# A two-layer recurrent block on one core: keys turned on TensorE, SSD scores by 64 keys, TensorE's rounds in a loop, and another order in the last pair

## Chip, core and metric

The kernel runs on one core of a Trainium2 chip. The metric is device time in microseconds (us) of one execution; lower is better. Several executions are timed and their median is given. One more execution is run under the hardware profiler, and every row below is from that one.

## What is computed

The input is 2048 tokens of 256 channels in fp32 (two sequences of 1024). Two layers follow each other, each a sequence mixer gated by a feed-forward network:

```
xn = layernorm(x);  x = x + rwkv6(xn) * silu(ffn_2to4(xn))     # layer 0
xn = layernorm(x);  x = x + ssd(xn)   * silu(ffn(xn))          # layer 1
```

Layer 0's mixer is RWKV-6 with 4 heads of 64: per head `y_t = r_t (S + u k_t v_t^T)` and `S = d_t S + k_t v_t^T`, with a decay `d_t` for each token and channel. Its hidden layer keeps the 2 largest of each 4 units. Layer 1's mixer is SSD: each of 8 heads of 64 channels owns 512/8 = 64 of the rows of a sequence flattened over token and head, in chunks; inside a chunk `scores = (C B^T) * L`, where `L` is the exponential of differences of a cumulative sum and zero for a key behind its query. Everything is fp32.

## The kernel before

The tokens go through in 8 tiles of 256. A round works on a pair: tile `a` in layer 0 and tile `b` (the one before it) in layer 1. There are nine rounds: the first (tile 0 in layer 0 alone), pairs 1 to 7, and a final one (tile 7 in layer 1 alone). Each of the five engines has its own program, `one(a, b)`, written out by hand in the order in which that engine does its work; semaphores tie the engines together. PSUM has 8 banks of 512 columns; the table `FILLS` lists which product goes into which bank in which order, `open_bank` waits until the bank's previous content is freed, `wait_filled` and `wait_freed` are the readers' waits. The counts that they wait for are constants, or expressions of a loop register where the rounds are in a loop. `passed` is a semaphore that nobody waits for; incrementing it gives a wait an instruction to sit on.

On SyncE, GpSimd, ScalarE and VectorE pairs 1 to 6 are a hardware loop (`Fori`), and pair 7 and the final round are written out behind it. On TensorE all nine rounds are written out (`for n in range(1, NT)`).

In a pair TensorE does, among much else and in this order: the feed-forward products of pair unit 2 (`project_p(a, 2, ...)`), `high_levels` (the intra-chunk products of layer 0 at distances 32 and 64; L1651 and L1707), `scores(0)` and `scores(1)` (L1763), `project_p(a, 3, ...)`, `states` (L2002), `within` (L1778), `chunk_states` (L1933, keys times values of layer 0 for the state), `across` (L1789), `outputs` (L1724 to L1735), and then the large feed-forward products of `b`. An fp32 product is two MATMUL records in the trace, a transpose one.

Layer 0's keys are kept by channel (`kT`); `chunk_states` needs them by token (`k0n`, which is the buffer `mixed_w`). In a pair this goes through VectorE and DRAM: `keys_to_end` (L1120 to L1123) writes the keys times their decay, transposes them by 32x32 blocks and SyncE's `key_rows` (L397, L400) stores them with 8 DMAs and loads them with one. In the first round TensorE transposes them instead (`keys_turned`, L1915).

`ssd_scores` multiplies, for each chunk of 128 rows and each sequence half `s`, all 128 keys with all 128 queries. The two halves `s` take different rows of the array (0 to 63 and 64 to 127). VectorE multiplies the result with `L` (`decayed_scores`, L1343) and frees the bank. The keys' side of a chunk is loaded from DRAM as rows: `cs_pos`, `Xrow` and `Brow` (the last two inside the buffer `hidB`), one DMA each.

In the first round TensorE runs `kept_busy` (L1967), 39 small products that nobody reads, ahead of `rank_mix` (L1816), which waits for VectorE's `rank_inputs` (L1174).

Of the kernel before, what the change touches and what calls it, by code (L numbers as in the profile page):

```python
# [17 lines left out]
F32 = mybir.dt.float32  # L18
# [6 lines left out]
P = 128  # L25
TOKENS, BATCH, C = 2048, 2, 256
T = 256
# [26 lines left out]
FILLS = [["mix_w", "dw", "w0", "mix_g0", "L0", "M0", "p3g", "kv", "F0"],  # L54
         ["p0g", "mix_k", "w1", "mix_g1", "L1", "M1", "p3u", "yT"],
# [5 lines left out]
         ["X1", "C0", "sc2", "ys0", "n1g", "n3g", "p1g"]]  # L61
BANKS = len(FILLS)
# [53 lines left out]
def build_block(nc, A):  # L116
    with ExitStack() as ctx:
# [3 lines left out]
        def sem(name):  # L121
# [4 lines left out]
             if n not in ("x", "out", "x_turned", "n_dram", "row_dram", "cs_dram", "b_dram", "x_dram", "k_dram", "w_mix2b", "w_dec2")}  # L126
# [64 lines left out]

        k0_turned = mixed["k"][:, :, :].rearrange("p a b -> p (a b)")
# [78 lines left out]
        k_blocks = sem("k_blocks")  # L271
        k_stored = sem("k_stored")
        k_rows = sem("k_rows")
# [99 lines left out]
        def _(sp_):  # L373
# [17 lines left out]
            def key_rows(a):  # L391
                wait(k_rows, a.count(16, 0))
                wait(k_blocks, a.count(1, 0))
                to = A["k_dram"].rearrange("(j a h i b) -> i h a j b", a=32, h=CH, i=4, b=32)
                for i in range(4):
                    for h in range(CH):
                        sp_.dma_start(to[i, h], k0_turned[32 * i:32 * i + 32, h * T:(h + 1) * T].rearrange(  # L397
                            "p (j b) -> p j b", b=32)).then_inc(k_stored, 16)
                wait(k_stored, a.count(128, 0))
                sp_.dma_start(k0n[:, :, :].rearrange("p a b -> p (a b)").rearrange("p (q c) -> p q c", q=NQ),  # L400
                              A["k_dram"].rearrange("(q p c) -> p q c", p=P, c=C)).then_inc(k_rows, 16)

# [29 lines left out]
            def one(a, b, last=False):  # L432
# [11 lines left out]
                if b:  # L444
# [3 lines left out]
                    wait(X_rows, b.count(16, 16))  # L448
# [4 lines left out]
                    wait(cs_loaded, b.count(48, 16))  # L453
# [4 lines left out]
                    sp_.dma_start(cs_pos[:, :], cs_dram.rearrange("(c p) -> p c", p=P),  # L458
                                  allow_slow_non_contiguous=True).then_inc(cs_loaded, 16)
# [5 lines left out]
                    sp_.dma_start(Xrow.rearrange("p q c d -> p (q c) d"),  # L465
# [1793 lines left out]
```

## Time and profile before

| | before |
|---|---|
| median of 3 runs | 716.09 us (715.89 to 716.32) |
| the profiled execution | 717.52 us |
| its span, first to last instruction | 715.7 us |
| TensorE (PE) busy | 702.5 us, 98% |
| TensorE weight loads (PEld) | 597.9 us, 84% |
| VectorE (DVE) busy | 496.1 us, 69% |
| ScalarE (ACT) busy | 338.1 us, 47% |
| GpSimd (POOL) busy | 76.7 us, 11% |
| granted TensorE clock | 1.000 of full speed |
| share of PE in the chain that ended last | 87% |

The profiled execution lies 1.4 us over the median and 1.8 us over its own span. Names of a row: line of the kernel, engine, operation, output<-inputs, shape, count. A start time is in us from the start of the span; the second number is the time from the group's first start to its last end. Ends of matmuls are modelled and overlap with the next, so the length of a piece of TensorE's work is read as the difference of two starts.

### The profile page before, as it was taken

What the parts mean: (1) busy time and instruction counts of PE and PEld (TensorE: products, weight loads), DVE (VectorE), ACT (ScalarE), POOL (GpSimd) and SP (SyncE); (2) the same over time, 40 slices, a digit from 0 to 9 for tenths busy, and PEclk for the clock granted to TensorE, in tenths of its full rate; (3) what the DMA queues carried; (4) which work ended last, traced back from release to release, by engine and by line L of the source; (5) the groups of instructions that cost most, each with busy time, mean ns of one, the idle gap of its engine ahead of it and who ended that gap; (6) DMA issues with size and microseconds to landing.
All of it is one profiled execution on the core that took longest, in us unless ns stands there. A gap on an engine that the chain in (4) does not pass through costs nothing.

```text
span 715.7 us, 18156 instructions
## 1 busy us (share of the span) xinstructions
PE 702.5 (98%) x7010; PEld 597.9 (84%) x7010; DVE 496.1 (69%) x1214; ACT 338.1 (47%) x671; POOL 76.7 (11%) x85
## 2 busy tenths in 40 slices
PE   7999999999999999999999999999999999999998
PEld 5777788888888788887888878888788888888887
DVE  5995988528884488755896568954789529895133
ACT  1423782147711586206852068421783237821790
POOL 6301011101110011100111001110011100110020
PEclk9999999999999999999999999999999999999999
DMA  7911460125501364012720236202370025601370
GB/s 231 408 44 30 136 103 18 22 82 143 96 2 30 102 128 83 16 30 89 149 61 16 52 120 110 47 15 74 104 128 23 16 77 136 105 12 25 122 120 16
DMA packets 139572, 59.46 MB, mean 83 GB/s; under 512 B 119728, under 2 KB 131312, under 8 KB 137968
## 3 DMA queue, kind: packets, MB, share of 16 engines
q1 hardware_dynamic: 139504, 58.44, 33.9%
q8 instruction: 57, 0.93, 0.6%
q14 instruction: 11, 0.09, 0.0%
HBM read 44.18 MB, written 14.24 MB: 82 GB/s over the span
## 4 chain that ended last, share of the span: by engine, by line
PE 87%; DVE 5%; issue 3%; DMA 2%; ACT 2%; SPq 1%; POOL 0%; DVEq 0%; POOLq 0%; ACTq 0%
PE psum L1542 68%; PE psum L1651 2%; PE psum L1763 2%; PE psum L1778 2%; ACT BC L626 1%; PE psum L1596 1%; PE psum L1621 1%; PE psum L1816 1%; PE psum L2002 1%; PE psum L1684 1%; PE psum L1863 1%; PE psum L1633 1%; PE psum L1789 1%; PE psum L1735 1%; PE psum L1724 1%
## 5 line engine op out<-in xcount | busy, mean ns | idle before, releaser
L626 ACT ACTIVATE BC<-psum 64x256 f32<-64x256 f32 x128 | 81.6, 637 | 1.9 <-PE psum L1542 0.2
L1542 PE MATMUL psum<-xn1T,sb_n_gate 128*128 128x256 f32 x256 | 61.3, 382 | 0.0
L1542 PE MATMUL psum<-xn1T,sb_n_up 128*128 128x256 f32 x256 | 60.5, 379 | 0.0
L1542 PE MATMUL psum<-xnT,sb_f_gate 128*128 128x256 f32 x240 | 57.8, 383 | 0.0
L1542 PE MATMUL psum<-xnT,sb_f_up 128*128 128x256 f32 x240 | 57.0, 379 | 0.0
L1542 PEld LDWEIGHTS psum<-xn1T,sb_n_gate 128*128 128x128 f32 x256 | 48.0, 190 | 6.8
L1542 PEld LDWEIGHTS psum<-xn1T,sb_n_up 128*128 128x128 f32 x256 | 48.2, 190 | 6.3
L757 ACT ACTIVATE thFB<-psum 128x512 f32<-128x512 f32 x8 | 4.8, 597 | 102.1 <-PE psum L1542 102.1
L1542 PEld LDWEIGHTS psum<-xnT,sb_f_up 128*128 128x128 f32 x240 | 45.2, 189 | 6.8 <-issue 0.3
L1542 PEld LDWEIGHTS psum<-xnT,sb_f_gate 128*128 128x128 f32 x240 | 44.7, 189 | 7.2 <-DVE xnT L1205 0.2
L1542 PE MATMUL psum<-sb_n_down,hidB 128*128 128x256 f32 x224 | 49.5, 379 | 0.0
L1542 PEld LDWEIGHTS psum<-sb_n_down,hidB 128*128 128x128 f32 x224 | 42.6, 190 | 5.8
L577 POOL TENSOR_SCALAR_AFFINE_SELECT cs_row<-cs_row 128x2048 f32<-128x2048 f32 x8 | 16.1, 2006 | 277.1 <-DVE xn_turned L1012 251.9
L1542 PE MATMUL psum<-sb_f_down,hid 128*128 128x256 f32 x192 | 42.4, 379 | 0.0
L1542 PEld LDWEIGHTS psum<-sb_f_down,hid 128*128 128x128 f32 x192 | 36.5, 190 | 5.0
L652 ACT ACTIVATE cs_row<-cs_row,cs_col 128x128 f32<-128x128 f32 x128 | 38.9, 392 | 0.0
L924 DVE SCALAR_TENSOR_TENSOR hid<-th,psum 128x512 f32<-128x512 f32 x23 | 15.7, 685 | 24.0 <-PE psum L1542 24.0
L1542 PE MATMUL psum<-sb_w_X,xn1T 128*128 128x256 f32 x128 | 31.9, 392 | 0.0
L583 POOL TENSOR_TENSOR cs_half<-cs_half,BC 128x1024 f32<-128x1024 f32 x8 | 19.1, 2383 | 115.4 <-ACT cs_half L721 115.4
L1542 PE MATMUL psum<-xn1T,sb_w_B 128*128 128x256 f32 x128 | 31.0, 385 | 0.2
L1542 PE MATMUL psum<-xn1T,sb_w_res 128*128 128x256 f32 x128 | 30.8, 385 | 0.0
L740 ACT ACTIVATE mixed_v<-mixed_k 128x512 f32<-128x512 f32 x8 | 5.0, 630 | 54.4 <-DVE mixed_k L1248 54.4
(265 smaller groups left out, 1494.4 us busy)
## 6 DMA issues: line engine op xcount, KB each, us to landing
cs_row<-cs_dram SPq DMA_DIRECT2D x8, 1024.0 KB, 5.0
x_dram<-gate SPq DMA_DIRECT2D x8, 512.0 KB, 2.8
cs_half<-cs_dram SPq DMA_DIRECT2D x16, 256.0 KB, 5.8
hidB<-x_dram SPq DMA_DIRECT2D x8, 512.0 KB, 5.7
b_dram<-B_turned SPq DMA_DIRECT2D x32, 128.0 KB, 3.5
hidB<-b_dram SPq DMA_DIRECT2D x8, 512.0 KB, 4.2
X<-in_x SPq DMA_DIRECT2D x9, 256.0 KB, 2.9
XT<-in_x_turned SPq DMA_DIRECT2D x8, 256.0 KB, 2.9
```

The costliest lines, as they stand in the source:

```text
L577: g.affine_select(out=cs_row[:, :, :], in_=cs_row[:, :, :], compare_op=ALU.is_ge, fill=NEG, base=0, pattern=[[0, NQ * SCH], [1, P]], chann ...
L583: g.tensor_tensor(cs_half[:, :], cs_half[:, :], BC[:, 1, :, :].rearrange("p t h -> p (t h)"), ALU.mult).then_inc(Cdec_ready, 1)
L626: ins = a_.activation(cols[:, par, 2 * pair:2 * pair + 2, :], src[64 * par:64 * par + 64, :, s, :], ACT.Identity)
L652: ins = a_.activation(cs_row[:, n, :], cs_row[:, n, :], ACT.Exp, bias=cs_col[:, n:n + 1])
L924: free(d.scalar_tensor_tensor(out=to, in0=buf[:, :], scalar=2.0, in1=ps(t, name + "u")[:, :], op0=ALU.mult, op1=ALU.mult), t, name + "u")
L1542: ins = t_.matmul(ps(t, name)[first_row:first_row + rows, col:col + n], w, x, start=(k == 0), stop=(k == len(ws) - 1))
L1596: ins = t_.matmul(ps(t, "F0")[:, q * C:(q + 1) * C], hid[:, m, q * P:(q + 1) * P], W["f_down"][:, m * C:(m + 1) * C], start=(m == 0 and q ...
L1621: ins = t_.matmul(ps(t, "mix_" + f)[:, h * T:(h + 1) * T], W["w_mix2a"][r, h * P:(h + 1) * P], aT[r, :], start=True, stop=True)
L1633: ins = t_.matmul(ps(t, f"mix_g{q}")[:, h * P:(h + 1) * P], W["w_mix2b"][r, h * P:(h + 1) * P], aT4[r, :], start=True, stop=True)
L1651: ins[e] = t_.matmul(lev_pair[64 * hf:64 * hf + 64, e, first + g * 32:first + (g + 1) * 32], keys[r, c:c + 64], q, start=True, stop=True)
L1763: ins[s] = t_.matmul(ps(t, names[s])[:, i * P:(i + 1) * P], Bf[r, c * P:(c + 1) * P], Cf[r, c * P:(c + 1) * P], start=True, stop=True)
L1778: t_.matmul(y_out(t, s, c, par), Xrow[:, s, c, :], m[:, par, :], start=(c == 0), stop=(c == 0), skip_group_check=True)
```

## The change

1. **Keys.** `keys_to_end`, `key_rows` and the buffer in DRAM go. In each pair TensorE transposes the keys (`keys_turned`) once VectorE has multiplied them with their decay (`last_update`), and ScalarE copies them from PSUM (`copy(a, k0n, "k0T", NQ)`).
2. **Scores.** Each chunk is done by 64 keys: the first 64 keys with all 128 queries, the last 64 with the 64 queries behind them. The output rows of odd chunks are exchanged, so the first half of one chunk and the second half of the next lie in the same rows of PSUM. Keys therefore stand in another order in odd chunks: `cs_pos`, `Xrow` and `Brow` are each loaded by three DMAs (`KEY_ROWS`) in place of one, and GpSimd masks `cs_row` with three operations in place of one.
3. **Order in a pair.** `high_levels` goes ahead of `project_p(a, 2, "g")`, `chunk_states` right behind the scores, `outputs` ahead of `across`. VectorE's order follows.
4. **Loop.** TensorE's pairs 1 to 6 are a hardware loop (`rounds(pe, one)`); 23 increments of `passed` ahead of `out_1` go.
5. **Pair 7.** `out_0` stands right behind `down_part(a, 1, 4, 8)`; ScalarE does `out_scaled` ahead of the sigmoid of the down product, VectorE `residual_0` ahead of `hidden_n(b, 2)`.
6. **First round.** `kept_busy` has 19 products in place of 39.

```diff
+KEY_ROWS = [(slice(0, P), 0, slice(0, P)), (slice(0, 64), 1, slice(64, P)), (slice(64, P), 1, slice(0, 64))]
...
@@ sync
-            def key_rows(a):
...
-                        sp_.dma_start(to[i, h], k0_turned[32 * i:32 * i + 32, h * T:(h + 1) * T].rearrange(
-                            "p (j b) -> p j b", b=32)).then_inc(k_stored, 16)
...
-                    sp_.dma_start(Brow.rearrange("p q c d -> p (q c) d"),
-                                  b_dram.rearrange("(c p d) -> p c d", p=P, d=SD)).then_inc(B_rows, 16)
+                    keys = b_dram.rearrange("(c two p d) -> p c two d", two=2, p=P, d=SD)
+                    for to, r, from_ in KEY_ROWS:
+                        sp_.dma_start(Brow.rearrange("p q (c two) d -> p (q c) two d", two=2)[to, :, r, :],
+                                      keys[from_, :, r, :]).then_inc(B_rows, 16)
                     if a:
-                        key_rows(a)
                         token_rows(a)
@@ gpsimd
-                    g.affine_select(out=cs_row[:, :, :], in_=cs_row[:, :, :], compare_op=ALU.is_ge, fill=NEG, base=0,
-                                    pattern=[[0, NQ * SCH], [1, P]], channel_multiplier=-1).then_inc(cs_masked, 1)
+                    for last, r, two, base in ((P, slice(0, P), 0, 0), (P, slice(0, P), 1, 64), (64, slice(0, 64), 1, -64)):
+                        m = by_two[r, :, two, :]
+                        ins = g.affine_select(out=m, in_=m, compare_op=ALU.is_ge, fill=NEG, base=base,
+                                              pattern=[[0, NQ * SCH // 2], [1, P]], channel_multiplier=-1)
...
@@ scalar
                     ffn_tanh(a, "p2", th[0], th_ready, "p0")
+                    copy(a, k0n[:, :, :], "k0T", NQ)
                     L_exps(1)
@@ vector
                     B_by_block(1)
-                    end_args()
+                    dve.wait_ge(out_stored, b.count(16, 16))
...
                     level_next(a, 5)
+                    end_args()
+                    low_taken(a)
                     gate_0()
-                    low_taken(a)
-                    keys_to_end(a)
+                    high_taken(a)
+                    last_update(a)
                     res_gate(0)
                     res_gate(1)
-                    high_taken(a)
-                    last_update(a)
                     decayed_scores(0)
-                    decayed_scores(1)
+                    states_0()
+                    B_decayed()
+                    for n in (2, 1, 3):
+                        decayed_scores(n)
                     hidden_p(a, 2)
-                    B_decayed()
...
                     states_1()
-                    states_0()
                     hidden_p(a, 3)
@@ tensor, ssd_scores
-                        ins[s] = t_.matmul(ps(t, names[s])[:, i * P:(i + 1) * P], Bf[r, c * P:(c + 1) * P],
-                                           Cf[r, c * P:(c + 1) * P], start=True, stop=True)
+                    for first in range(2):
+                        k, at = slice(c * P + 64 * first, c * P + 64 * first + 64), 64 * (first ^ (c % 2))
+                        for s in range(NQ):
+                            r = half_rows(s)
+                            ins[s] = t_.matmul(ps(t, names[s])[at:at + 64, i * P + 64 * first:(i + 1) * P], Bf[r, k],
+                                               Cf[r, c * P + 64 * first:(c + 1) * P], start=True, stop=True)
@@ tensor, one, last pair
                         close_bank(down_part(a, 1, 4, 8), a, "F0")
+                        out_0()
                         up_n(b, 2)
-                        out_0()
                         gate_n(b, 3)
                     up_n(b, 3)
-                    for _ in range(23):
-                        pe.sem_inc(passed, 1)
                     out_1()
...
-                    kept_busy(["mix_w", "mix_k"], 39)
+                    kept_busy(["mix_w", "mix_k"], 19)
...
-            one(Tile(None, 0, first=True), None)
-            for n in range(1, NT):
-                one(Tile(None, n), Tile(None, n - 1))
-            one(None, Tile(None, NT - 1, last=True))
+            rounds(pe, one)
```

TensorE's program in a pair, before, from `project_p(a, 2, "u")` to the start of `outputs` (counts are products; `thFB,xn` and `rT,kT` are `high_levels`, `BC` the scores, `hidB` the states):

```order
L1542 MATMUL psum<-xnT,sb_f_up 128x256 x4
L1542 MATMUL psum<-xnT,sb_f_gate 128x256 x4
L1651 MATMUL psum<-thFB,xn 64x32 x16
L1707 MATMUL psum<-rT,kT 64x64 x8
L1763 MATMUL psum<-BC 128x128 x16
L1542 MATMUL psum<-xnT,sb_f_gate 128x256 x4
L1542 MATMUL psum<-xnT,sb_f_up 128x256 x4
L2002 MATMUL psum<-hidB 64x64 x14
L1778 MATMUL psum<-cs_row,hidB 64x64 x32
L1933 MATMUL psum<-v,mixed_w 64x64 x8
L1789 MATMUL psum<-cs_half,S 64x64 x28
L1724 MATMUL psum<-S,rT 64x64 x16
```

The same place in the changed program, inside the loop, up to the first chunk of the scores:

```order
L1535 MATMUL psum<-xnT,sb_f_up 128x256 x4
L1524 REGISTER_ALU
L1663 REGISTER_ALU
L1644 MATMUL psum<-thFB,xn 64x32 x16
L1694 REGISTER_ALU
L1700 MATMUL psum<-rT,kT 64x64 x8
L1535 MATMUL psum<-xnT,sb_f_gate 128x256 x4
L1912 MATMUL psum<-ident,kT 128x128 x4
L1760 MATMUL psum<-BC 64x128 x2
L1760 MATMUL psum<-BC 64x64 x2
```

`high_levels` now has a dense product on either side, four transposes are new, and a chunk's 2 products of 128 keys are 4 of 64 keys, 2 of them with 64 queries. Instructions on registers are new: there are 37 of them and 7 waits written as ISA instructions in a round.

VectorE's program at the same place, before (L1010 and L1012 make level 5, L1033 and L1027 are `low_taken`, L1120 to L1123 `keys_to_end`, L1311 `res_gate`):

```order
L1210 SCALAR_TENSOR_TENSOR gT<-gT,psum 128x512
L1033 COPY_PREDICATED own<-masks,psum 128x128x2
L1033 COPY_PREDICATED own<-masks,psum 128x64x4
L1033 COPY_PREDICATED own<-masks,psum 128x32x8
L1027 COPY_PREDICATED own<-masks,psum 128x8x16 x2
L1116 REGISTER_ALU
L1120 TENSOR_TENSOR mixed_w<-kT,dec 128x4x64
L1121 COPY mixed_w<-kT 128x4x64
L1123 STREAM_TRANSPOSE mixed_k<-mixed_w 128x512
L1309 ISA
L1311 SCALAR_TENSOR_TENSOR gate<-gate,psum 128x512 x2
```

And in the changed program, from `low_taken` on:

```order
L1030 COPY_PREDICATED own<-masks,psum 128x8x16 x2
L1196 SCALAR_TENSOR_TENSOR gT<-gT,psum 128x512
L339 REGISTER_ALU
L1036 COPY_PREDICATED own<-masks,psum 128x8x32
L999 TENSOR_TENSOR kT<-kT,dec 128x4x64
L1000 TENSOR_TENSOR rT<-rT,dec 128x4x64
L1295 ISA
L1297 SCALAR_TENSOR_TENSOR gate<-gate,psum 128x512 x2
L334 REGISTER_ALU
L1329 TENSOR_TENSOR cs_row<-cs_row,psum 128x512
L1207 SCALAR_TENSOR_TENSOR S<-S,dec,psum 128x64 x4
```

The transpose and one copy are gone, the gate stands behind `low_taken`, and the states of layer 0 (L1207, before L1221) come right behind the first `decayed_scores`.

## Rows read from the trace of the kernel before

**Rows 1.** The page's first part: busy us (share of span) xinstructions

```profile
PE 702.5 (98%) x7010; PEld 597.9 (84%) x7010; DVE 496.1 (69%) x1214; ACT 338.1 (47%) x671; POOL 76.7 (11%) x85
```

**Rows 2.** Timeline of PE, pair 4: start us, us, what, [idle before <-releaser]

```profile
359.86 0.67 PE L1651 MATMUL psum<-thFB,xn 64*64 64x32 f32 x32
360.95 2.06 PE L1763 MATMUL psum<-BC 64*128 64x128 f32 x32
362.93 2.00 PE L1542 MATMUL psum<-xnT,sb_f_gate 128*128 128x256 f32 x8
...
366.59 1.03 PE L2002 MATMUL psum<-hidB 128*64 128x64 f32 x28
...
369.35 0.65 PE L1933 MATMUL psum<-v,mixed_w 128*64 128x64 f32 x16
369.92 1.05 PE L1789 MATMUL psum<-cs_half,S 64*64 64x64 f32 x56
371.16 0.69 PE L1724 MATMUL psum<-S,rT 64*64 64x64 f32 x32 [0.18 <-DVE S L1221]
```

**Rows 3.** Timeline of PE, pair 4: four transposes between dense products

```profile
388.36 0.60 PE L1610 MATMUL psum<-ident,mixed_k 128*128 128x128 f32 x4
388.80 1.89 PE L1542 MATMUL psum<-xn1T,sb_n_up 128*128 128x256 f32 x8
```

**Rows 4.** Timeline of PE, pair 4: products of 64 rows by 64 columns with 96 columns

```profile
348.36 0.89 PE L1684 MATMUL psum<-rU,kT 64*64 64x96 f32 x32
349.07 0.62 PE L1651 MATMUL psum<-mixed_r,mixed_w 64*64 64x32 f32 x32
```

**Rows 5.** Timeline of PE, pair 1: the wait for the turned keys

```profile
107.86 2.07 PE L1778 MATMUL psum<-cs_row,hidB 128*64 128x64 f32 x64
110.67 0.69 PE L1933 MATMUL psum<-v,mixed_w 128*64 128x64 f32 x16 [0.75 <-DMA mixed_w<-k_dram]
```

**Rows 6.** Timeline of DVE, pair 4: the gate and the end of `low_taken`

```profile
355.80 0.69 DVE L1210 SCALAR_TENSOR_TENSOR gT<-gT,psum 128x512 f32<-128x512 f32 x1 [0.38 <-ACT gT L714]
...
358.10 0.50 DVE L1027 COPY_PREDICATED own<-masks,psum 128x128 f32<-128x128 int8 x2
```

**Rows 7.** Timeline of ACT, pair 4: `L_exps(1)`

```profile
363.00 2.44 ACT L652 ACTIVATE cs_row<-cs_row,cs_col 128x128 f32<-128x128 f32 x8
```

**Rows 8.** Timelines at the end of pair 4: PE around the 23 increments and at the round's end, then ACT

```profile
393.98 1.89 PE L1542 MATMUL psum<-xn1T,sb_n_up 128*128 128x256 f32 x8
395.71 3.62 PE L1542 MATMUL psum<-sb_w_sout,gate 128*128 128x256 f32 x16
...
412.99 1.02 PE L1816 MATMUL psum<-mixed_w,sb_w_mix 128*128 128x256 f32 x4
...
406.27 0.60 ACT L757 ACTIVATE thFB<-psum 128x512 f32<-128x512 f32 x1 [13.14 <-PE psum L1542]
```

**Rows 9.** Timelines of PE and of DVE, first round

```profile
10.41 1.36 PE L1967 MATMUL psum<-ident 64*64 64x32 f32 x78
11.71 1.13 PE L1816 MATMUL psum<-mixed_w,sb_w_mix 128*128 128x256 f32 x4
...
10.06 1.04 DVE L1174 SCALAR_TENSOR_TENSOR mixed_w<-dxT,sb_vecs,xnT 128x256 f32<-128x256 f32 x2
```

**Rows 10.** Timelines of PE in pair 7 and the final round, and of DVE in the final round

```profile
650.35 1.99 PE L1542 MATMUL psum<-sb_w_rkvgo,mixed_w 128*128 128x256 f32 x8 [0.60 <-DVE mixed_w L1268]
...
666.47 0.63 PE L1805 MATMUL psum<-xn1T,sb_w_dt 128*32 128x128 f32 x8 [0.32 <-DMA xn1T<-n_dram]
...
697.67 1.03 PE L2002 MATMUL psum<-hidB 128*64 128x64 f32 x28
...
700.97 1.05 PE L1789 MATMUL psum<-cs_half,S 64*64 64x64 f32 x56 [0.37 <-issue]
...
695.33 1.16 DVE L1333 TENSOR_TENSOR hidB<-hidB,to_end 128x448 f32<-128x448 f32 x2 [1.20 <-DMA hidB<-b_dram]
```

**Rows 11.** DMA issues: out<-in, count, KB each, median us from issue to landing

```profile
n_dram<-xn_turned SPq DMA_DIRECT2D x56, 32.0 KB, 1.7
```

More of the change, by code:

```diff
@@ L125, in build_block @@
         W = {n: sb("sb_" + n, list(A[n].shape)) for n in A
-             if n not in ("x", "out", "x_turned", "n_dram", "row_dram", "cs_dram", "b_dram", "x_dram", "k_dram", "w_mix2b", "w_dec2")}
+             if n not in ("x", "out", "x_turned", "n_dram", "row_dram", "cs_dram", "b_dram", "x_dram", "w_mix2b", "w_dec2")}
         W["w_mix2b"], W["w_dec2"] = sb("sb_mix2b", [NQ * DMIX, C]), sb("sb_dec2", [NQ * DDEC, C])
@@ L447, in one @@
                     sp_.sem_inc(passed, 1)
-                    wait(X_rows, b.count(16, 16))
+                    wait(X_rows, b.count(48, 16))
                     sp_.dma_start(x_dram.rearrange("(q p n) -> p q n", q=NQ, p=P), Xnat).then_inc(X_stored, 16)
@@ L452, in one @@
                     sp_.sem_inc(passed, 1)
-                    wait(cs_loaded, b.count(48, 16))
+                    wait(cs_loaded, b.count(80, 16))
                     wait(cs_rows_loaded, b.count(16, 16))
@@ L464, in one @@
                     wait(X_stored, b.count(16, 32))
-                    sp_.dma_start(Xrow.rearrange("p q c d -> p (q c) d"),
-                                  x_dram.rearrange("(c p d) -> p c d", p=P, d=SD)).then_inc(X_rows, 16)
-                    wait(B_rows, b.count(16, 16))
+                    keys = x_dram.rearrange("(c two p d) -> p c two d", two=2, p=P, d=SD)
+                    for to, r, from_ in KEY_ROWS:
+                        sp_.dma_start(Xrow.rearrange("p q (c two) d -> p (q c) two d", two=2)[to, :, r, :],
+                                      keys[from_, :, r, :]).then_inc(X_rows, 16)
+                    wait(B_rows, b.count(48, 16))
                     wait(B_blocks, b.count(2, 2))
@@ L802, in one @@
                     ffn_tanh(b, "n1", thB[1], None)
-                    ffn_tanh_0()
-                    out_scaled()
-                    ffn_tanh(b, "n2", thB[0], None, "n0")
+                    if a.reg is not None:
+                        ffn_tanh_0()
+                        out_scaled()
+                        ffn_tanh(b, "n2", thB[0], None, "n0")
+                    else:
+                        ffn_tanh(b, "n2", thB[0], None, "n0")
+                        out_scaled()
+                        ffn_tanh_0()
                     ffn_tanh(b, "n3", thB[1], None, "n1")
@@ L1757, in ssd_scores @@
                     open_bank(t, name)
+                    pe.sem_inc(passed, 1)
                 ins = [None] * NQ
@@ L1799, in one @@
             def one(a, b):
-                first_a, first_b = not b, a and b and b.off == 0
+                first_a, first_b = not b, a and b and (a.reg is not None)
                 def steps_product(bank, h):
@@ L1938, in outputs @@
                     wait_freed(pe, a, "kv")
-                    if a.first:
-                        wait_freed(pe, a, "L0")
-                    wait_freed(pe, a, "L1" if a.first else "M1")
+                    for e in range(2):
+                        wait_freed(pe, a, f"{'L' if a.first else 'M'}{e}")
                     pe.wait_ge(q0_ready, a.count(1, 1))
@@ L2048, in one @@
                     project_p(a, 2, "u")
+                    high_levels(a)
                     project_p(a, 2, "g")
-                    high_levels(a)
+                    keys_turned()
                     scores(0)
                     scores(1)
+                    chunk_states()
                     project_p(a, 3, "g")
@@ L2056, in one @@
                     within()
-                    chunk_states()
+                    outputs()
                     across()
-                    outputs()
                     ffn_n(b, 0)
```

87 lines of the change are left out of this document (32 added, 55 removed).

## The prediction

> **What bounds the kernel now.** I read the page's first part first: TensorE (PE) is busy 98% of the span and no other engine over 69% [rows 1]. So the question is what TensorE's own program costs, and where it waits. Next comes TensorE's timeline of one pair in the middle, where the reader is to see that each group starts as the one before it lets go: two dense groups lie 1.73 us apart [rows 8], and the only idle time in the part that the change rewrites is 0.18 us ahead of `outputs` [rows 2]. [...] Then come the waits that occur once: 0.75 us in pair 1 [rows 5], 0.60 us in pair 7 and 0.32 us and 0.37 us in the final round [rows 10], and the products of the first round that only keep the engine busy [rows 9]. All that the other engines do is hidden, as long as it isn't late.
>
> **The change in a pair, part by part.**
>
> *Scores.* The 32 records take 360.95 to 362.93, 1.98 us [rows 2]. The new ones are 64 records of 64 rows by 64 columns, half with 128 queries and half with 64, 96 in the mean. The nearest row has just that shape and 96 columns: 32 records in 0.71 us, 22 ns each [rows 4]. 64 of them give 1.42 us, which is the lower bound. The upper bound is that a 64-query product doesn't run beside the 128-query products of its neighbour chunk; then a chunk takes what its 128-query products take, as now, 1.98 us. The rows of odd chunks are exchanged, so each quarter of the array gets 128 and 64 queries in turn, and I take the lower bound plus 0.1 for entering from a dense product: 1.5 us, that is -0.5.
>
> *Transposes.* Four transposes between dense products cost 388.80 - 388.36 = 0.44 us [rows 3]: +0.44. They stand on the path, since all of TensorE's program does.
>
> *Order.* `high_levels` now has dense products on both sides. What entering and leaving costs is read from the two dense groups between scores and states: 366.59 - 362.93 = 3.66 us where twice 1.73 is 3.46: +0.20. It could be nothing, if the scores behind the transposes start as quickly as they now do behind `high_levels`, or 0.3. `chunk_states` costs 369.92 - 369.35 = 0.57 us [rows 2] wherever it is, and I take it as moved for nothing. `outputs` no longer follows `chunk_states` through VectorE's update of the state, so its 0.18 us of waiting and what goes with it end: -0.2.
>
> Sum of a pair: -0.5 + 0.44 + 0.20 - 0.2 = -0.06 us; for seven pairs -0.4. Bounds of a pair: -0.35 to +0.55.
>
> *What hides the rest.* Each new wait has to be met in time. (1) `high_levels` wants its banks 1.73 us earlier, at about 358.1. VectorE's `low_taken` ends at 358.10 + 0.50 = 358.60, but the gate (0.69 us, 0.38 us idle ahead of it) goes behind it [rows 6], so it ends near 357.6: met with some 0.4 us to spare. (2) The transposes want the keys at about 361. `high_levels` ends near 359.2 (it lasts 1.09 us [rows 2]), and VectorE needs two operations of some 0.4 us behind it; met by a dense group. (3) `chunk_states` wants ScalarE's copy at about 363. The copy goes ahead of `L_exps(1)`, which starts at 363.00 now [rows 7] and could start two microseconds earlier, since `high_levels` ends that much earlier; the scores (1.5 us) cover the copy's 0.6. If that cover were gone, 0.6 us a pair would show. (4) The 9 DMAs of the keys leave SyncE's queue; in their place 2 each are added for `cs_pos`, `Xrow` and `Brow`. In a pair these land behind work of several microseconds. GpSimd's mask, three operations in place of one, ends ahead of `end_args`, which now stands behind level 5. All at nothing. (5) VectorE loses a transpose and a copy (1.0 us), so nothing behind it gets later.
>
> *Pair 1.* There `chunk_states` waits 0.75 us for the keys from DRAM, and starts 2.81 us behind `within` [rows 5]; the DMA goes: -0.8.
>
> *The loop.* I cost it at nothing. TensorE's instructions are issued ahead of the engine: the 23 semaphore increments between 393.98 and 395.71 leave no gap, the distance is the 1.73 us of a dense group [rows 8]. The same hides the 44 register instructions and ISA waits of a round, and means that taking the 23 away gains nothing. The last wait ahead of the branch back is for the bank that ScalarE's L757 frees at 406.27 + 0.60 = 406.87; the engine is busy with what was issued until 412.99 [rows 8]. So a stall of the branch stays hidden up to 6.1 us.
>
> [...]
>
> *First round.* 78 records of `kept_busy` run from 10.41, and `rank_mix` starts at 11.71; VectorE has its input ready at 10.06 + 1.04 = 11.10 [rows 9]. With half of the products `rank_mix` can start 0.1 to 0.2 us behind 11.10: -0.4. At worst nothing is left of it (a later wait for VectorE in that round), at best 0.6.
>
> *Pair 7.* `out_0` waits 0.60 us for the gated output now [rows 10], and `out_scaled` stands behind the sigmoid (0.6 us) on ScalarE. Ahead of it the input is ready that much earlier, but `out_0` is wanted 1.73 us earlier too, so part of the wait stays: -0.3. The whole chain behind it (residual, norm, turn, DRAM) starts some 2 us earlier, and so the final round's first wait, 0.32 us for `xn1T` [rows 10], ends: -0.3.
>
> *Final round.* The scores are 0.5 us shorter here too, but this round is fed by DMA: VectorE idles 1.20 us for `Brow`, has it decayed at 695.33 + 1.16 = 696.49, and TensorE starts the states at 697.67 [rows 10]. Three DMAs in place of one for `Brow` (and for two loads ahead of it in the same queue) may land 0 to 1.5 us later. And `across` waits 0.37 us for VectorE's chain of states already. I take -0.1, between -0.5 and +1.0.
>
> **Sum.** -0.4 (seven pairs) - 0.8 - 0.4 - 0.6 - 0.1 = -2.3 us. The profiled execution took 717.52 us, so 715.2 in its place; it lies 1.4 us over the median, and the median of the changed kernel should be 716.09 - 2.3 = 713.8 us.
>
> **The rivals.** What can be told from no change here is 0.2%, 1.4 us: faster is below 714.7, slower above 717.5.
>
> *The forecast's mechanism, with more gain.* The pairs come out 0.3 us shorter each (scores at 1.42 us, no cost of entering and leaving): -2.1 more, 711.7 us. For it: TensorE is the bound, and what it saves counts in full. Against it: the transposes are paid in each pair. Chance 0.14.
>
> *The same.* The pair costs 0.2 us more than I have it (a wait for ScalarE's copy or more time at each change of shape), seven times +1.4 us: 715.2 us; or the final round loses 1.0 to `Brow` and the first round gives nothing: the same place. Chance 0.24.
>
> *Slower: the small products of a chunk don't run beside the large ones.* Place: `ssd_scores`. Twice as many products, a chunk takes what its 128-query products take, 1.98 us, and the transposes come on top. +0.48 us in eight rounds, +3.8: 717.6 us. It decides from about 0.46 us a round on. For it: one product follows the other in program order, and unequal neighbours occur in no row. Against it: products on different quarters overlap fully when they are equal (22 ns a record [rows 4]). Chance 0.12.
>
> *Slower: the branch back isn't hidden.* Place: TensorE between `project_p` of the next tile and `rank_mix`. [...] It decides once 0.8 us shows at each branch. [...] Against it: 6.1 us of cover. Chance 0.10.
>
> *The forecast.* 713.8 us, by itself 712.7 to 714.6. Chance 0.40.
>
> **How the numbers follow.** Faster: 0.40 + 0.14 = 0.54. Within 0.2%: 0.24. Slower: 0.12 + 0.10 = 0.22. The range leaves out the unhidden branch above and the far end of the largest gain below: 711.3 to 717.8 us.
>
> **What the changed profile would show.** The scores' group starts and the next group starts 1.5 us later (right) or 2.0 us later (the third rival). Four transposes of `kT` in a pair with 0.44 us to the next start and no idle time ahead of them, nor ahead of `chunk_states`. The distance from `project_p(a, 2, "u")` to the first dense product behind `across` within 0.3 us of today's. No idle time at the loop's branch: `rank_mix` 1.73 us behind the last dense group's start. No wait for a DMA in pair 1. `rank_mix` of the first round near 11.3. In the final round the states right behind the dense group, or idle with `hidB<-b_dram` as the releaser. The prediction is wrong if idle time shows in each pair, since everything there counts seven times.

## The result, and the profile after

The changed kernel takes **718.85 us**, the median of 5 executions (718.06 to 720.36), beside 716.32 us for the kernel before, timed again next to it in 5 executions (715.89 to 717.66): ratio **1.0033, 95% interval 1.0019 to 1.0047**. It is slower, where I forecast faster. The profiled execution took 718.1 us (span 716.4) beside 717.52 (span 715.7), so of the 2.5 us between the medians the two spans show 0.7.

The page's first part, of the kernel after:

```profile
PE 703.2 (98%) x7254; PEld 596.2 (83%) x7254; DVE 491.9 (69%) x1200; ACT 343.2 (48%) x678; POOL 85.9 (12%) x101
```

This answers to [rows 1]: TensorE is the bound as before, at 98%. GpSimd has more to do. Next, TensorE's timeline of the kernel after: a branch back, pair 4, and pair 7 (start, duration, line, shapes, and in brackets idle time with what ended it).

```profile
149.23 1.71 PEld L1535 LDWEIGHTS psum<-xnT,sb_f_gate 128*128 128x128 f32 x8
149.44 1.90 PE L1535 MATMUL psum<-xnT,sb_f_gate 128*128 128x256 f32 x8
...
150.96 1.70 PEld L1535 LDWEIGHTS psum<-xnT,sb_f_up 128*128 128x128 f32 x8
151.17 1.89 PE L1535 MATMUL psum<-xnT,sb_f_up 128*128 128x256 f32 x8
...
153.16 0.51 PEld L1813 LDWEIGHTS psum<-mixed_w,sb_w_mix 128*128 128x128 f32 x3 [0.50 <-issue]
153.17 0.69 PE L1813 MATMUL psum<-mixed_w,sb_w_mix 128*128 128x256 f32 x2
...
356.33 1.90 PE L1535 MATMUL psum<-xnT,sb_f_up 128*128 128x256 f32 x8
358.34 0.67 PE L1644 MATMUL psum<-thFB,xn 64*64 64x32 f32 x32
358.82 0.68 PE L1700 MATMUL psum<-rT,kT 64*64 64x64 f32 x16
359.44 2.00 PE L1535 MATMUL psum<-xnT,sb_f_gate 128*128 128x256 f32 x8
361.27 0.60 PE L1912 MATMUL psum<-ident,kT 128*128 128x128 f32 x4
361.80 1.57 PE L1760 MATMUL psum<-BC 64*64 64x128 f32 x64
363.30 0.69 PE L1926 MATMUL psum<-v,mixed_w 128*64 128x64 f32 x16
363.92 2.00 PE L1535 MATMUL psum<-xnT,sb_f_gate 128*128 128x256 f32 x8
...
615.58 1.89 PE L1535 MATMUL psum<-xnT,sb_f_up 128*128 128x256 f32 x8
617.99 0.67 PE L1644 MATMUL psum<-thFB,xn 64*64 64x32 f32 x32 [0.52 <-DVE own L1030]
```

Two lines of the kernel before belong beside them, the dense groups ahead of `high_levels` and ahead of `rank_mix` in pair 4; the next groups start at 359.86 [rows 2] and at 412.99 [rows 8]:

```profile
358.03 1.89 PE L1542 MATMUL psum<-xnT,sb_f_gate 128*128 128x256 f32 x8
...
411.26 1.89 PE L1542 MATMUL psum<-xnT,sb_f_up 128*128 128x256 f32 x8
```

Three things are to be seen. (a) `rank_mix` (L1813) stands 153.17 - 151.17 = 2.00 us behind the last dense group's start, where the kernel before has 412.99 - 411.26 = 1.73. At the five branches back the distance is 2.00, 2.19, 1.94, 1.78 and 1.84 us, and the four first products behind each take 0.10 us longer; at the sixth, which isn't taken, it is 1.73. Together 1.09 + 0.50 = 1.6 us. (b) `high_levels` (L1644) starts 2.01 us behind the start of a dense group that lets go after 1.82 (so it was in all seven pairs of the kernel before, 359.86 - 358.03 above); over the seven pairs it is 2.27, 2.02, 2.00, 2.01, 2.00, 1.99 and 2.41, 2.0 us in all. (c) The rest of pair 4 is what I forecast: scores 1.50 us, transposes 0.53.

```profile
L364 ACTq COMPARE_BRANCH  x6: 40/45/53, 151.5 to 584.7; - x6
L364 PEldq COMPARE_BRANCH  x6: 83/3682/3983, 149.1 to 582.3; - x6
```

And the register instruction ahead of TensorE's last dense group before the first branch, the only one of line L1524 from 146 to 150 us:

```profile
L1524 PEldq ALU_OP  x1: 32/32/32, 147.3 to 147.3; - x1
```

TensorE's branch back takes 3.6 to 4.0 us when it is taken, and 0.08 the sixth time. ScalarE's, with a shorter body, takes 0.05.

And where (b) comes from, VectorE and GpSimd in the timeline of the kernel after, in pair 4 and then pair 7:

```profile
351.38 1.31 DVE L1312 STREAM_TRANSPOSE B_turned<-BC 128x512 f32<-128x512 f32 x2 [0.33 <-DVE own L1099]
352.61 0.72 DVE L1013 TENSOR_TENSOR xn<-thB,dec 128x256 f32<-128x256 f32 x1
...
353.45 0.41 DVE L1013 TENSOR_TENSOR thFB<-xn_turned,dec 128x256 f32<-128x256 f32 x1
...
357.46 0.50 DVE L1030 COPY_PREDICATED own<-masks,psum 128x128 f32<-128x128 int8 x2
...
611.96 1.12 DVE L1013 TENSOR_TENSOR xn<-thB,dec 128x256 f32<-128x256 f32 x1
```

```profile
349.40 1.09 POOL L571 TENSOR_SCALAR_AFFINE_SELECT cs_row<-cs_row 128x1024 f32<-128x1024 f32 x1 [38.10 <-DVE xn_turned L1015]
350.72 2.33 POOL L571 TENSOR_SCALAR_AFFINE_SELECT cs_row<-cs_row 128x1024 f32<-128x1024 f32 x2 [0.23 <-POOL cs_row L571]
...
609.24 3.56 POOL L571 TENSOR_SCALAR_AFFINE_SELECT cs_row<-cs_row 128x1024 f32<-128x1024 f32 x3 [38.32 <-DVE xn_turned L1015]
```

The same place in the kernel before, GpSimd in pair 4:

```profile
349.45 2.01 POOL L577 TENSOR_SCALAR_AFFINE_SELECT cs_row<-cs_row 128x2048 f32<-128x2048 f32 x1 [37.88 <-DVE xn_turned L1012]
```

The mask lasted until 351.46; in three operations it lasts until 353.05 in pair 4 and 612.80 in pair 7. VectorE's first product of level 4, 0.42 us by itself, starts ahead of that end, and each time ends 0.28 us behind it: 353.33 and 613.08. (0.28 is less than 0.42: either a part of it was done beside the mask, or GpSimd's ends are recorded late; no run tells which.) What is late there is late in `low_taken` too, which ends at 357.46 + 0.50 = 357.96; `high_levels` starts 0.38 us behind that.

### The profile page after: what moved, and what is told of

The parts are those of the page before. It is cut to its first block, busy times and chain, and to the rows that moved or that the text cites. A ratio compares the mean times of both kernels' runs of the same rounds, so it can differ in the third digit from the quotient of the medians.

```text
span 716.4 us, 18704 instructions
## 1 busy us (share of the span) xinstructions
PE 703.2 (98%) x7254; PEld 596.2 (83%) x7254; DVE 491.9 (69%) x1200; ACT 343.2 (48%) x678; POOL 85.9 (12%) x101
## 4 chain that ended last, share of the span: by engine, by line
PE 91%; DVE 5%; issue 2%; ACT 1%; POOL 0%; DVEq 0%; POOLq 0%; ACTq 0%
PE psum L1535 71%; PE psum L1644 2%; PE psum L1775 2%; PE psum L1760 2%; PE psum L1614 1%; PE psum L1813 1%; PE psum L1994 1%; PE psum L1786 1%; PE psum L1589 1%; PE psum L1677 1%; PE psum L1860 1%; PE psum L1626 1%; PE psum L1926 1%; PE psum L2173 1%; PE psum L1717 1%
## 5 line engine op out<-in xcount | busy, mean ns | idle before, releaser
L571 POOL TENSOR_SCALAR_AFFINE_SELECT cs_row<-cs_row 128x1024 f32<-128x1024 f32 (+1 forms) x24 | 26.2, 1092 | 283.2 <-DVE xn_turned L1015 253.3
```

Of the source, the lines that this page charges most:

```text
L571: ins = g.affine_select(out=m, in_=m, compare_op=ALU.is_ge, fill=NEG, base=base, pattern=[[0, NQ * SCH // 2], [1, P]], channel_multiplier=-1)
```

## The experiments

Theory: two things that I had put at nothing cost the time, the branch back on TensorE and the longer mask on GpSimd. Rivals: the body of a pair or the final round lost it, or the branch only shows in a profile. The runs were made in three batches, each beside the kernel before: 716.51 us in the first (part 1), 716.69 in the second (e4, e5, e7, e2h) and 716.47 in the third (e8 to e11). A difference of 0.2 us between runs of two batches says nothing.

**1. The loop.** The changed kernel again, written out, and hinted; and the loop alone in the kernel before.

> The changed kernel once more, beside the others on their chip: 718.9 us if the five timed executions were typical. In its first profile the five distances from the last dense group to rank_mix behind a branch back were 2.00, 2.19, 1.94, 1.78 and 1.84 us where 1.73 is the bare distance. If the stall is a fetch whose length varies, the new profile has other values at the same five places and all other distances unchanged to 0.05 us; if the loss lies in the body (the new wait ahead of high_levels, the final round), it repeats where it was.

> The changed kernel with TensorE's rounds written out again (nothing else undone). Theory (the branch back shows): the five places lose their excess, 1.09 us of distance and 5 x 0.10 us of slower first products in the profiled execution, up to 3.4 us if the timed executions stalled longer than the profiled one: 715.5 to 717.2 us, and executions as close together as those of the kernel before. Rival (the body of the pair and the final round cost it): no change, 718.5 to 719.0 us.

```diff
-            rounds(pe, one)
+            one(Tile(None, 0, first=True), None)
+            for n in range(1, NT):
+                one(Tile(None, n), Tile(None, n - 1))
+            one(None, Tile(None, NT - 1, last=True))
```

(three conditions that tell the first and the last pair by the loop's register go back to the tile's number with it)

> The kernel before with TensorE's rounds in a loop and nothing else (the 23 increments stay). Theory: the branches cost here what they cost in the changed kernel, 1.6 to 3.4 us: 717.9 to 719.7 us, spread over more than 1 us. Rival (body): 716.3 us. My prediction, loop at nothing: 716.3 us too.

```diff
-            one(Tile(None, 0, first=True), None)
-            for n in range(1, NT):
-                one(Tile(None, n), Tile(None, n - 1))
-            one(None, Tile(None, NT - 1, last=True))
+            rounds(pe, one)
```

(with the same three conditions by the register)

```diff
-        def rounds(eng, one):
+        def rounds(eng, one, **loop):
...
-            with eng.Fori(1, NT - 1) as it:
+            with eng.bass.Fori(1, NT - 1, engines=[eng.engine], **loop) as it:
...
-            rounds(pe, one)
+            rounds(pe, one, hint_back_edge=True)
```

Only TensorE's loop gets the hint.

| run | median us (executions) | ratio to before | interval |
|---|---|---|---|
| after_again | 718.35 (12) | 1.0024 | 1.0014 to 1.0035 |
| e1_unrolled | 721.99 (6) | 1.0063 | 1.0042 to 1.0084 |
| e2_loop_alone | 720.98 (6) | 1.0061 | 1.0041 to 1.0080 |
| e3_hint | 716.34 (12) | 1.0000 | 0.9990 to 1.0011 |

The hint gives back 2.0 us, as expected, and the loop alone makes the kernel before slower, by 4.5 us, which is more than I expected (717.9 to 719.7): the branch costs time. In after_again the five distances are 1.82, 2.25, 2.06, 2.11 and 1.91 us: the same places, other values, 1.5 us over the bare distance and 0.5 for the slower first products, 2.0 in all. The source line of the loop in e3_hint:

```profile
L364 PEldq BRANCH_PREFETCH_HINT  x6: 31/31/50, 65.2 to 494.4; - x6
L364 PEldq COMPARE_BRANCH  x6: 80/220/260, 148.9 to 580.4; - x6
```

The branch takes 0.22 us, `rank_mix` is 1.73 us behind the dense group at all five places, and the excess is gone. So the stall was the wait for the target's instructions, not the branch or its registers. The part of the page on DMA queues, first of the kernel after, then of e3_hint, says the same:

```profile
q8 instruction: 67, 1.10, 0.7%
```

```profile
q8 instruction: 22, 0.36, 0.2%
```

Without the hint a fetch starts 1.3 us behind each taken branch (150.38 us, branch at 149.12; it lands at 151.47, and the branch is over at 152.92, 1.45 us later), and blocks are fetched all through the loop; with it no instruction DMA of TensorE appears between 116.45 and 582.08 us.

But e1_unrolled missed my expectation: written out, the changed kernel is the slowest of all. Its timeline and its windows in pair 4 (windows: busy time and count of each engine, granted clock, DMA share):

```profile
350.12 0.52 PE L1644 MATMUL psum<-xn_turned,thB 64*64 64x32 f32 x22
352.37 0.41 PE L1644 MATMUL psum<-xn_turned,thB 64*64 64x32 f32 x10 [1.73 <-issue]
352.72 2.69 PE L1535 MATMUL psum<-xn1T,sb_w_res 128*128 128x256 f32 x8
```

```profile
350.00:352.00 2.00, 0.64 (x44) 0.53 (x36) 1.67 (x4) 1.97 (x4) 1.62 (x3) 1.00 0.06 8
352.00:354.00 2.00, 1.63 (x16) 1.44 (x17) 1.85 (x6) 1.95 (x4) 0.78 (x1) 0.97 0.31 49
354.00:356.00 2.00, 2.00 (x6) 1.61 (x5) 1.90 (x7) 0.83 (x2) 0.00 (x0) 0.50 0.68 98
```

In the middle of a level TensorE waits 1.73 us for nothing but its own instructions, up to 352.37; an instruction DMA was on its way from 349.62 to 350.99, so the work goes on 1.38 us behind its landing, much as at the branch (1.45). Behind that idle time the granted clock is 0.50 in 354 to 356 us, and the dense groups are 2.49 and 2.76 us apart where they are 1.83 and 1.73 at 1.00: another 1.7 us. An idle time of 1.21 us at 636 us in the same profile left it at 1.00.

Why there? The kernel before has 57 instruction DMAs of 16 KB for 14543 instructions on TensorE's queues, e1_unrolled 58 for 14894. That is 255 and 257 each; I take it as 256 (an estimate from these counts). A written-out round of the kernel before has 1792 instructions, 7 x 256, and its seventh fetch starts 72.0 to 72.8 us behind `rank_mix` in each of pairs 1 to 7: each round meets its fetches at about the same places. One of e1_unrolled has 1844, and the places walk by 52 a round (the seventh fetch at 74.5, 70.5 and 66.5 us in pairs 1 to 3), now and then into a stretch of small products.

**2. The mask, and its order on VectorE**, all on the hinted version (716.34 us).

> The hinted version of the changed kernel, with end_args moved from ahead of low_taken to behind it on VectorE (0.45 us of VectorE's time: 353.87 to 354.32 in the hinted profile). Theory (VectorE is late with low_taken, TensorE waits ahead of high_levels): the distance from project_p(a, 2, u) to the first product of high_levels falls from 1.99 to 1.82 us in six pairs, and in pair 7 from 2.41 to about 1.96: -1.4 us against the hinted version's 716.3, so 714.9 us. Rival (the wait moves to the next thing that VectorE owes, the gate or the update of level 6): 716.0 to 716.4 us.

```diff
-                    end_args()
                     low_taken(a)
+                    end_args()
                     gate_0()
```

> The hinted version with GpSimd's mask in one operation as before; the rows of odd chunks are then masked at the wrong places, so the output differs. Theory (GpSimd's three operations last 3.65 us instead of 2.01, reach into VectorE's first tensor_tensor of level 4, and hold it: 0.72 us in a middle pair and 1.11 in pair 7 where 0.42 is its time): that operation is 0.42 us again, VectorE is 0.3 us earlier in a pair and 0.7 in pair 7, and the wait ahead of high_levels goes: 714.6 to 715.0 us. Rival (the longer operation has another cause, such as its own operands): still 0.72 us, 716.3 us.

```diff
-                    for last, r, two, base in ((P, slice(0, P), 0, 0), (P, slice(0, P), 1, 64), (64, slice(0, 64), 1, -64)):
...
+                    g.affine_select(out=cs_row[:, :, :], in_=cs_row[:, :, :], compare_op=ALU.is_ge, fill=NEG, base=0,
+                                    pattern=[[0, NQ * SCH], [1, P]], channel_multiplier=-1).then_inc(cs_masked, 1)
```

> The hinted version, with GpSimd's second mask operation over queries 0 to 63 only (there is nothing to mask behind them for those keys): 512 columns in place of 1024 in that operation, the output as in the reference. Theory (the mask's third operation reaches into VectorE's first tensor_tensor of level 4 and makes low_taken late): the three end 0.5 us sooner, at about VectorE's start in a middle pair and 0.15 us into it in pair 7, so the operation takes 0.42 us again, the distance from project_p(a, 2, u) to high_levels is 1.82, and the time is that of the run with one mask, 714.7 us. Rival (something else in that run, such as its exp of other values, made it quick): 716.3 us.

```diff
-                        m = by_two[r, :, two, :]
+                        n = 64 if base == 64 else P
+                        m = by_two[r, :, two, 0:n]
...
-                                              pattern=[[0, NQ * SCH // 2], [1, P]], channel_multiplier=-1)
+                                              pattern=[[0, NQ * SCH // 2], [1, n]], channel_multiplier=-1)
```

e4_end_args: 720.16 us (6 executions; ratio 1.0045, 1.0032 to 1.0058), 3.8 us slower than e3_hint. Both expectations missed the time; the rival had it right that the wait moves, but it moves to what ScalarE owes, and grows. Its chain of waits, the first row, and a row of ScalarE's timeline:

```profile
PE psum L1912 <- ACT other L728: 3.4, 7, 0.9
```

```profile
358.05 0.21 ACT L733 ACTIVATE to_end<-to_end 128x16 f32<-128x16 f32 x1 [2.05 <-DVE to_end L1305]
```

`high_levels` no longer waits, but ScalarE stands 2.05 us idle for `end_args`, its exps and `other` copy come later, and the transposes wait for those. Both users of this stretch of VectorE are near their limit.

e5_one_mask: 714.65 us (9 executions; ratio 0.9972, 0.9962 to 0.9982), as expected; by itself it leaves open that other values made it quick, which the next run rules out. e8_hint_narrow_mask: **714.82 us** (713.96 to 715.59, 9 executions; ratio to the kernel before **0.9972, 0.9959 to 0.9984**), as expected too. GpSimd, VectorE and TensorE in the timeline of e8_hint_narrow_mask, pair 4:

```profile
349.19 1.89 POOL L572 TENSOR_SCALAR_AFFINE_SELECT cs_row<-cs_row 128x512 f32<-128x512 f32 x2 [0.23 <-POOL cs_row L572]
...
351.08 0.38 DVE L1014 TENSOR_TENSOR xn<-thB,dec 128x256 f32<-128x256 f32 x1
...
355.58 0.49 DVE L1031 COPY_PREDICATED own<-masks,psum 128x128 f32<-128x128 int8 x2
...
354.80 1.89 PE L1536 MATMUL psum<-xnT,sb_f_up 128*128 128x256 f32 x8
356.63 0.67 PE L1645 MATMUL psum<-thFB,xn 64*64 64x32 f32 x32
```

The mask ends at 351.08, VectorE's operation starts then and takes 0.38, and `high_levels` follows after 1.83 us; so it is in six pairs. In pair 7 the mask (606.80 to 609.92) still reaches into that operation, which takes 0.68 us, and the distance is 1.97 where I expected 1.82. Only half of one operation's columns was taken away; that it gives 1.5 us shows the collision, not GpSimd's work, to be the cost. This version beats both kernels.

**3. The terms that I had counted.**

> The hinted version with the scores by 128 keys, and with them the single DMAs and the single mask: the rest of the change alone. Theory (the scores give 0.48 us in each of eight rounds, 3.9 us, and their mask takes 1.5 us back through VectorE): 716.3 + 3.9 - 1.5 = 718.7 us, with no wait ahead of high_levels. Rival (what the scores give is lost behind them, in states, within or the final round): 716.5 to 717.2 us.

```diff
-                    for first in range(2):
...
-                            ins[s] = t_.matmul(ps(t, names[s])[at:at + 64, i * P + 64 * first:(i + 1) * P], Bf[r, k],
-                                               Cf[r, c * P + 64 * first:(c + 1) * P], start=True, stop=True)
+                    for s in range(NQ):
+                        r = half_rows(s)
+                        ins[s] = t_.matmul(ps(t, names[s])[:, i * P:(i + 1) * P], Bf[r, c * P:(c + 1) * P],
+                                           Cf[r, c * P:(c + 1) * P], start=True, stop=True)
```

(with one DMA each for `cs_pos`, `Xrow` and `Brow`, and the single mask, as in the kernel before)

> The kernel before with TensorE's loop and the hint, nothing else. Theory (the loop costs only the branch, and with the hint that takes 0.2 us and is hidden): 716.3 us, 715.8 if the instruction fetches that the hinted loop no longer shows had cost something. Rival (the register instructions of the loop cost too): 716.8 to 717.5 us. With e7 it gives the keys' part: e7 minus this is what transposes, order and pair 7 are worth; by my terms (+0.44 + 0.2 - 0.2 in a pair, -0.8, -0.4, -0.6) this is +1.3 us.

Its edit is that of e2_loop_alone and that of e3_hint together.

> The kernel before without its 23 semaphore increments, its only edit; rounds stay written out. My prediction (they are hidden, taking them away gains or costs nothing): 716.5 us. Rival: with them a written-out round is 1792 instructions, 7 x 256, and each instruction DMA brings 16 KB, 256 instructions, so each round meets its fetches at the same places; without them they drift by 23 instructions a round and fall, as in the run with the changed kernel written out (1844 a round), into stretches of small products: 717.5 to 719.5 us with idle time put down to issue.

```diff
-                    for _ in range(23):
-                        pe.sem_inc(passed, 1)
```

> e8_hint_narrow_mask with pair 7's order as before on TensorE, ScalarE and VectorE. By my term (0.3 for out_0 and 0.3 for xn1T) it is 0.6 us slower than that one: 715.3 us. By the profiles so far the new order is worth 0.1 to 0.3 us only, since out_0 still waits and the final round waits for the next thing: 714.9 us.

TensorE's part of its edit; ScalarE and VectorE go back in the same way:

```diff
-                        out_0()
                         up_n(b, 2)
+                        out_0()
                         gate_n(b, 3)
```

> e8_hint_narrow_mask with 39 rounds of kept_busy in the first round instead of 19. By my term it is 0.4 us slower: 715.1 us. Rival (rank_mix starts when its input is ready, whatever stands ahead of it): 714.7 us; rank_mix then starts as late with 19 as with 39, counted from the start of kept_busy.

```diff
-                    kept_busy(["mix_w", "mix_k"], 19)
+                    kept_busy(["mix_w", "mix_k"], 39)
```

| run | median us (executions) | ratio to before | interval |
|---|---|---|---|
| e7_old_scores | 718.23 (11) | 1.0020 | 1.0011 to 1.0029 |
| e2h_loop_hint_alone | 717.14 (12) | 1.0006 | 0.9997 to 1.0014 |
| e9_before_no_incs | 717.16 (12) | 1.0005 | 0.9995 to 1.0016 |
| e10_old_pair7 | 715.52 (12) | 0.9984 | 0.9974 to 0.9994 |
| e11_kept_busy_39 | 716.32 (12) | 0.9995 | 0.9985 to 1.0006 |

- *Scores.* e7_old_scores and e5_one_mask differ in the scores and their loads and share the single mask: 718.23 - 714.65 = 3.6 us, 0.45 a round. In its timeline the old form takes 363.40 - 361.42 = 1.98 us again, against 1.50.
- *Keys, order, first round, pair 7.* e7_old_scores minus e2h_loop_hint_alone is +1.1 us; my terms gave +1.3.
- *The loop with the hint.* e2h_loop_hint_alone came out at 717.14 us, in the range of its rival (register instructions cost), not at 716.3. But beside the 716.69 of its batch that is +0.45 with an interval from -0.2 to +1.0, and its profile (716.85 us) isn't longer than that of the kernel before: whether the registers cost anything is not shown.
- *The 23 increments.* By the time, taking them away makes no difference that can be told. The profile of e9_before_no_incs has more idle time put down to issue than the kernel before (1.8 us in five waits against 1.0 in four), so both expectations are in part right: the fetches do walk (the seventh of a round starts 73.9 us behind `rank_mix` in pair 1, then 77.0, 78.4, 80.7, 83.8 and 85.7 us), and mostly miss the small products here.
- *Pair 7's order.* +0.7 us without it, by the medians (0.6 by the profiles). With the old order `out_0` waits 0.60 us again; with the new one it still waits, 646.37 - 644.37 = 2.00 us against 1.73. That is worth 0.5 us where I had 0.3. The wait for `xn1T` shows in neither run, so its 0.3 us isn't in this difference. Another 0.25 us stands at pair 7's scores (1.79 us in e10_old_pair7 for 1.50), which the edit doesn't touch.
- *kept_busy.* e11_kept_busy_39 is 1.5 us slower, not 0.4. From the first of these products to `rank_mix` it is 1.29 us with 39 rounds and 0.73 with 19, and of these 0.56 us 0.10 are lost again to a later wait: 0.46. There is a second place, in pair 7, behind the loop, where all code has moved by 20 products and their loads. The fetch there ran from 605.97 to 607.07:

```profile
607.39 0.41 PE L1645 MATMUL psum<-xn_turned,thB 64*64 64x32 f32 x15
608.38 0.47 PE L1645 MATMUL psum<-xn_turned,thB 64*64 64x32 f32 x17 [0.58 <-issue]
```

The two profiles differ by 0.7 us in all (715.31 and 714.61), so of the 1.5 us between the medians 0.8 stand in no trace.

## Why the prediction was wrong, step by step

**Failed: "I cost it at nothing ... a stall of the branch stays hidden up to 6.1 us" (the loop).** The cover was mis-sized. I counted from the last wait ahead of the branch to the end of the engine's work, as if the sequencer were at the branch as soon as that wait ends. It comes there at 149.12, when 16 weight loads and 17 matmul records are still to start, some two dense groups, which end at 151.17 + 1.89 = 153.06: 3.9 us of cover. The branch takes 3.6 to 4.0 us (3682 ns in the middle), so it is nearly hidden and shows by 0.05 to 0.52 us. My rival of the branch that isn't hidden had the place, but needed 0.8 us at each branch to decide; shown are 0.3 to 0.4 in the mean in the two profiles, and 2.0 us in all by the medians (718.35 to 716.34). Of the 3.7 us of a taken branch the instruction DMA is 1.1 (150.38 to 151.47, the branch at 149.12). That all of those 6.1 us could be in hand was my estimate; the traces show less. In six profiles (after, after_again, e2, e2h, e3, e8), hinted or not, the same 16 loads and 17 matmul records are still to start at each of the 36 branches. The register instruction ahead of the last dense group, L1524 at 147.30, stands 1.83 us ahead of the branch with the same 33 in hand. So the sequencer was at no wait there: it followed the engine at the pace of its dense groups, 33 ahead. If as many are in hand in a stretch of small products, whose records lie 22 ns apart in [rows 4], 17 records are 0.4 us of cover (an estimate), and a fetch there shows sooner: 1.73 us in e1_unrolled at 352 us.

**Failed: "GpSimd's mask, three operations in place of one ... All at nothing", and with it "(1) ... met with some 0.4 us to spare".** I asked only whether the mask is in time for `end_args`. It is, but it reaches into VectorE's level 4, which makes VectorE 0.3 us later in a middle pair and 0.7 in pair 7, and the spare time of `high_levels` was smaller than that. The 0.4 us to spare were mis-sized too. Without the collision `low_taken` does end where I had it (356.07 in e8, 1.27 us behind the start of the dense group), but from its end to the first product of `high_levels` 0.38 us go by (357.96 to 358.34), which I had at nothing: 1.82 - 1.27 - 0.38 = 0.17 us were left. Shown by e8 and e5: 1.5 and 1.7 us; the distances above had 2.0. Beside the mask two kinds of VectorE's operations fare differently: the tensor_tensor (two inputs) ends 0.28 us behind the mask (not the 0.42 that it takes by itself, as said above), while the two transposes ahead of it (one input) take 1.31 us beside the mask, and as long in the kernel before, where all but 0.04 us of them lies behind its end (they start at 351.42, it ends at 351.46). What makes the difference, no run shows.

**Right, in size too.** Scores -0.5 a round (0.48 by the rows, 0.45 by the times). `high_levels` between dense groups +0.20 (1.83 and 1.84 in place of 1.73 at its two sides in e8). The pair: from the first product of `first_levels` to the transposes of the gated output (348.36 and 388.36 in the kernel before, [rows 4] and [rows 3]) e8 takes 39.98 us where the kernel before takes 40.00 or 40.18, -0.09 in the mean of pairs 2 to 6 (forecast -0.06). Pair 1: 40.06 for 40.92, -0.86 (-0.8 and the pair's -0.06). First round -0.46 by the profiles (-0.4).

**Right in the sum, partly by luck.** Pair 7: -0.7 by the medians for -0.6. `out_0` gave 0.5 and not 0.3. The final round's first wait is gone (0.32 us in the kernel before, none after), but it is as much gone in e10_old_pair7 with the old order, so the new order didn't earn that 0.3; the 0.25 us at the scores that fill the sum have no cause that a run shows.

**Off in size, small.** A transpose group costs 0.53 us (+0.44 forecast): behind it now stand the scores, not a dense group. `outputs` gave 0.3 us, not 0.2. The final round lost 0.3 us in the kernel after (49.51 us from its first product to the end for 49.24) where I had -0.1: its scores are 0.48 us shorter, but `Brow` is there 29.6 us behind the round's start, not 28.9, and VectorE waits 1.76 us for it, not 1.20. Its decayed scores end only at 698.80, and `within` starts 1.16 us behind the states, not 0.86; `across` waits 0.51 us, put down to issue. In e8 `Brow` came at 29.2 and the round took 49.06 us, -0.2: the term was near. The granted clock, 1.000 over the span of the kernel before, is 0.99 in its last stretch (664 to 716 us); nothing hangs on it.

Taken together: forecast -2.3, measured +1.8 to +2.5. Of these 4.1 to 4.8 us the branch is 2.0, the mask 1.5 to 1.7, and the rest isn't told apart. With both mended the change is worth 714.82 - 716.47 = -1.65 us, 0.65 short of the sum; the interval of the ratio (-2.9 to -1.1 us) holds -2.3.

**Open.** Why most timed executions of e2_loop_alone lie above its profile: it was profiled at 718.86 us and timed at a median of 720.98, and e2h_loop_hint_alone at 716.85 and 717.14. So the branches cost 2.0 us by the profiles and 3.8 by the medians there. In after_again, with the same loop unhinted, it isn't so (718.43 and 718.35); what differs in the executions that weren't profiled, no trace shows.

## What to carry to other kernels

A loop on the engine that is the bound needs its branch's price beside its cover, and the cover is what the engine has in hand when its sequencer reaches the branch (here 3.9 us beside 3.6 to 4.0), not the distance to the last wait (6.1). Give the loop the hint for its branch back (2.0 us here). When an operation on GpSimd gets longer, look at what VectorE starts before its new end: being in time for its reader wasn't enough here (1.5 us). In code that is written out, an edit that changed the number of instructions moved the fetches behind it in three runs, and could cost at a place that it doesn't touch: 0.58 us in e11_kept_busy_39, 1.73 us and the clock behind it in e1_unrolled, and nothing that the time tells in e9_before_no_incs.

## What the runs showed that I had not expected

- With the hint, the loop of 1883 instructions on TensorE ran its later rounds without one instruction DMA in the trace; without it blocks were fetched in each round (67 against 22 packets). That fetched blocks can stay had not occurred to me.
- An idle time of 1.73 us behind small products was followed by a granted clock of 0.50 in 354 to 356 us, and cost as much again. The stalls at the branches, up to 0.52 us, left the clock at 1.00.
- The sequencer stood 33 records (16 loads, 17 matmuls) ahead of the engine at each of 36 branches, whatever the kernel. In dense groups (8 loads and 8 matmuls each) that is 3.9 us of cover.
- Writing the rounds out was the dearest form of the changed kernel, 5.7 us above the hinted loop, though it has no branch at all.
